# First layer of a four-layer program: reloads of the weights issued two units ahead, and each half's moves put on one queue

## The chip, the cores and the metric

The kernel runs on one core of one Trainium2 chip. The time is the device time of one execution in microseconds (us). For the kernel before it is 3445.14 us, the median of three runs (3443.86 to 3448.17).

## What is computed

The program chains four layers. The change touches the first alone, an attention over projected columns:

```python
def _L0_xattn_ref(z1ss, u1ss, Wqkv0, Wqkv1, Winj0, Winj1, Wo, bo, r_w_bias):
    for i in range(2):                       # columns 0:256 and 256:512
        h = jnp.einsum('od,bdl->bol', Wq_list[i], z1ss[:, :, s:e])
        h = h + jnp.einsum('od,bdl->bol', Wi_list[i], u1ss[:, :, s:e])
    q, k, v = jnp.split(w_heads, 3, axis=1)  # 16 heads of 64
    rq = q + r_w_bias[None, :, :, None]
    score = jnp.einsum('bndi,bndj->bnij', rq, k) * SCALE
    prob = jax.nn.softmax(score, axis=-1)
    attn_vec = jnp.einsum('bnij,bndj->bndi', prob, v)
    attn_out = jnp.einsum('od,bdl->bol', Wo, attn_vec) + bo[None, :, None]
    x = attn_out + z1ss
    return (x - m) * jax.lax.rsqrt(var + LN_EPS)
```

Here x is 8 x 256 x 512 in float32. The other three layers (a recurrent mixing layer, two attentions with a perceptron, a non-local block) run after it and are the same in both kernels.

## The kernel before

The function `l0_attention` works through 64 units. A unit n is one pair of heads (8 pairs) of one batch (8 batches). Batches go in four turns of two lanes, and the order of the units is turn, pair, lane: `where(n)` gives (turn bp, pair, lane l). All products are split into a high and a low part of float32r, so the weights of one pair are two tiles of 1 MB, `w_hi` and `w_lo` (two buffers each, by the pair's parity), and the weights for the values of two pairs are `wv_hi` and `wv_lo` (1 MB each, one buffer).

**Weights.** In turn 0 SyncE loads the raw weights, ScalarE and VectorE split them, and SyncE stores both parts to HBM (`split_weights`, L318 to L331). For turns 1 to 3 ScalarE reloads the parts (`load_w`, L685). A pair is counted over all turns as t = 8 bp + pair; its projection of q and k (L419) runs one unit ahead, inside unit 2t - 1. Before, the high parts (of `w`, and for even t of `wv`) are issued in unit 2t - 3 and the low parts in unit 2t - 2, both behind the second pair of exponentials.

**Turning the probabilities.** A unit's probabilities are made in two halves f = 0, 1 (two blocks of 128 rows each). VectorE transposes 32 x 32 blocks inside a half (L778), and 16 DMAs, called pieces here, move blocks between partitions from `prob` to `probT` (`move`, L270). A piece is 64 KB. Halves are numbered i = 2n + f and three buffers go round (`RING`). A piece may be issued when the half is transposed (`turned`) and the product that read the same `probT` buffer three halves ago is complete. Before, nine of a half's 16 pieces are issued by SyncE and seven by GpSimd. `half_moved` waits for both, on TensorE ahead of the product with the values (`weigh_values`, L478) and on ScalarE ahead of writing a `prob` buffer again (`exponentials`, L576).

**Order on each engine.** Each engine has one program in a fixed order. In unit n:

- TensorE: scores of blocks 0 and 1 (L453), projections of q and k for unit n + 1 (L419), scores of blocks 2 and 3, the turned row sums of unit n - 1 (L462), the output projection of n - 2 (L492), the product with the values of n - 1 (L478; first half, then second half, into one bank), and where pair is even the values of unit n + 1 (L437).
- ScalarE: exponentials of blocks 0 and 1, `q_hi` of n + 1 (L599), other copies, exponentials of blocks 2 and 3, the reload issues, the copy `oT` of the product of n - 1 (L612).
- GpSimd: scaling of the product of n - 2 (L380, waits for ScalarE's `oT`), the row sums of n - 1 (L375), the pieces of half 1 of unit n - 1, the pieces of half 0 of unit n.
- SyncE: its pieces of half 0 and of half 1 of unit n; then in turn 0, lane 0, `split_weights` of the next pair; loads of x and loads and stores of `acc` where a turn begins or ends.

GpSimd's pieces of half 1 of unit n thus stand behind the scaling of the product of unit n - 1. DMAs that ScalarE issues appear on queue q10 of the profile, SyncE's on q1, GpSimd's on q0.

Of the kernel before, what the change touches and what calls it, by code (L numbers as in the profile page):

```python
# [6 lines left out]
F32 = mybir.dt.float32  # L7
# [11 lines left out]
LANES = 2  # L19
TURNS = B // LANES  # L20
# [134 lines left out]
def l0_attention(nc, kept, first, d, x, u, att, x1):  # L155

    D, HP = 64, 8
# [3 lines left out]
    RING = 3  # L161
# [3 lines left out]
    QUADS = HP // 2  # L165
    MOVES = [(g, r) for g in range(Q) for r in range(Q)]
    BY_SP = 9
    H2 = range(2)
# [30 lines left out]
    w_scratch = [scratch(f"kept_w_{part}", (HP, P, KT, 2, 2, P)) for part in ("hi", "lo")]  # L199
    wv_scratch = [scratch(f"kept_wv_{part}", (QUADS, P, KT, 2, 2, P)) for part in ("hi", "lo")]  # L200

    with Phase(nc, "l0") as ph:
# [4 lines left out]
        w_hi, w_lo = [[ph.sb(f"w_{part}{i}", [P, KT, 2, 2, P], F32R) for i in range(2)] for part in ("hi", "lo")]  # L207
# [57 lines left out]
        def half_moved(eng, i):  # L265

            eng.wait_ge(moved_sp[i % RING], 16 * BY_SP * (i // RING + 1))
            eng.wait_ge(moved_pool[i % RING], 16 * (len(MOVES) - BY_SP) * (i // RING + 1))

        def move(eng, n, f, pieces, moved):  # L270

            i = 2 * n + f
            eng.wait_ge(turned, IT * n + 2 * f + 2)
            if i >= RING:
                full(eng, S[f"o{(i - RING) // 2}"])
            elif i == 1:
                eng.wait_ge(wv_lo_ready, 1)
            elif i == 2:
                eng.wait_ge(wo_lo_ready, 1)
            for g, r in pieces:  # L280
                eng.dma_start(probT[i % RING][r * SQ:(r + 1) * SQ, g, :, :, :, :],  # L281
                              prob[i % RING][g * SQ:(g + 1) * SQ, r * IT:(r + 1) * IT, :, :, :]).then_inc(moved[i % RING], 16)

        def projected(eng, n):

            full(eng, S[f"v{n}_1"] if where(n)[1] % 2 == 0 else S[f"k{n}"])

        with ph.block() as block:
            @block.sync
            def _(sp):  # L290
# [43 lines left out]
                for n in range(HALF):  # L334
                    bp, pair, l = where(n)
                    move(sp, n, 0, MOVES[:BY_SP], moved_sp)
                    move(sp, n, 1, MOVES[:BY_SP], moved_sp)
                    if bp == 0 and l == 0 and pair + 1 < HP:
# [23 lines left out]
            def _(pool):  # L362
# [19 lines left out]
                for n in range(HALF + 2):  # L382
# [4 lines left out]
                    if 0 < n <= HALF:  # L387
                        move(pool, n - 1, 1, MOVES[BY_SP:], moved_pool)
                    if n >= HALF:
                        continue  # L390
                    move(pool, n, 0, MOVES[BY_SP:], moved_pool)
                    if n == VAR + 1:
# [174 lines left out]
            def _(act):  # L567
# [116 lines left out]

                def load_w(t, part):  # L685
                    p, i = t % HP, t % 2
                    projected(act, LANES * (t - 2) + 1)
                    if i == 0:
                        act.wait_ge(wv_stored, 32 * QUADS)
                        act.dma_start((wv_hi, wv_lo)[part][:, :, :, :, :].bitcast(F32), wv_scratch[part][p // 2]).then_inc(wv_in, 16)  # L690
                    act.wait_ge(w_stored[i], 32 * QUADS)
                    act.dma_start((w_hi, w_lo)[part][i][:, :, :, :, :].bitcast(F32), w_scratch[part][p]).then_inc(w_in[i], 16)

# [14 lines left out]
                for n in range(HALF):  # L708
                    bp, pair, l = where(n)
                    exponentials(n, (0, 1))  # L710
                    if n + 1 < HALF:
                        queries(n + 1)
# [6 lines left out]
                    exponentials(n, (2, 3))  # L719
                    t = (n - 1) // LANES + 2  # L720
                    if HP <= t < TURNS * HP:
                        load_w(t, 1 - l)
                    if n == 0:
# [2507 lines left out]
```

## Time and profile before

| what | value |
|---|---|
| median of three runs | 3445.14 us (3443.86 to 3448.17) |
| the profiled execution | 3442.56 us |
| its span, first to last instruction | 3440.5 us |
| mean granted clock of TensorE | 0.949 |
| TensorE matmul busy | 3115.6 us, 91% |
| VectorE busy | 2362.2 us, 69% |
| ScalarE busy | 1742.2 us, 51% |
| GpSimd busy | 701.2 us, 20% |
| the first layer's 64 units | from the start to about 1302 us |

The page gives busy time by engine over the whole span; the first layer is a third of it. Rows of the trace name the line and the tile that an instruction writes and reads, what the engine waited for ahead of it, and for DMAs the time from issue to landing. "PE" is TensorE, "DVE" VectorE, "ACT" ScalarE, "POOL" GpSimd, "SP" SyncE; a "q" behind the name is the engine's sequencer, which issues DMAs.

### The profile page before, as it was taken

The numbers are of one execution on the slowest core, as the hardware profiler recorded it, in microseconds if no ns is written. First come the engines' busy times: TensorE is split into PE (matmuls) and PEld (weight loads), VectorE is DVE, ScalarE is ACT, GpSimd is POOL, SyncE is SP. The second block draws the span as 40 slices with busy tenths as digits, with TensorE's granted clock in tenths as the row PEclk, the third lists the DMA queues.
The fourth block names the chain that finished last, engine by engine and source line by source line (L and its number), as shares of the span: only waits on it lengthen the run. The fifth ranks groups of instructions, "written<-read, shape, count | busy, mean of one in ns | idle before, by whom it ended". The sixth has DMA issues, their size and how long they took to land. (4 is left out here: it accounts for less than half of the span.)

```text
span 3440.5 us, 55581 instructions
## 1 busy us (share of the span) xinstructions
PE 3115.6 (91%) x20384; PEld 2400.2 (70%) x20384; DVE 2362.2 (69%) x3589; ACT 1742.2 (51%) x4185; POOL 701.2 (20%) x1207
## 2 busy tenths in 40 slices
PE   7998999999998996799999997589999999699998
PEld 6777777777777774566666664378887787488885
DVE  6776666666675662999999999257777888543212
ACT  4454444544454543355566553247777777432222
POOL 2444444544444441000000000011101111000000
PEclk9999999999999998899999998789999999899999
DMA  7668766666675655445555444210011110310004
GB/s 245 209 218 268 225 184 183 207 212 197 197 234 162 207 143 187 121 96 123 116 117 120 104 109 104 59 64 14 26 56 56 44 44 29 108 50 12 25 13 167
DMA packets 179676, 434.78 MB, mean 126 GB/s; under 512 B 52912, under 2 KB 61104, under 8 KB 154960
## 3 DMA queue, kind: packets, MB, share of 16 engines
q1 hardware_dynamic: 120256, 262.17, 26.9%
q10 hardware_dynamic: 28304, 106.09, 8.6%
q0 software_dynamic: 30848, 62.97, 7.3%
q8 instruction: 164, 2.69, 0.3%
q14 instruction: 104, 0.85, 0.1%
HBM read 233.95 MB, written 62.91 MB: 86 GB/s over the span
## 5 line engine op out<-in xcount | busy, mean ns | idle before, releaser
L281 POOL DMA_DIRECT2D l_probT<-l_prob x896 | 441.2, 500 | 258.6 <-DVE l_prob L778 238.8
L756 DVE TENSOR_REDUCE l_nmax<-l_bank 128x1 f32<-128x512 f32 x512 | 317.0, 681 | 198.2 <-PE l_bank L453 198.2
L576 ACT ACTIVATE l_prob<-l_bank,l_nmax 128x512 f32<-128x512 f32 x512 | 344.5, 688 | 135.1 <-DVE l_nmax L756 120.5
L419 PE MATMUL l_bank<-l_x_hi,l_w_hi 128*128 128x256 f32 x1024 | 307.6, 300 | 75.4 <-DMA l_w_lo<-kept_w_lo 54.5
L778 DVE STREAM_TRANSPOSE l_prob<-l_prob 128x1024 f32<-128x1024 f32 x256 | 314.4, 1228 | 16.3 <-DVE l_acc L799 9.7
L419 PE MATMUL l_bank<-l_x_hi,l_w_lo 128*128 128x256 f32 x1024 | 299.8, 293 | 0.0
L419 PE MATMUL l_bank<-l_x_lo,l_w_hi 128*128 128x256 f32 x1024 | 299.0, 292 | 0.0
L1817 DVE TENSOR_TENSOR_SCAN l_kv<-l_wx,l_kv 128x2056 f32<-128x2056 f32 x64 | 283.8, 4435 | 3.1 <-DVE l_sxc L1938 1.5
L419 PEld LDWEIGHTS l_bank<-l_x_hi,l_w_hi 128*128 128x128 f32 x1024 | 207.0, 202 | 99.5 <-DMA l_w_lo<-kept_w_lo 59.2
L2391 ACT ACTIVATE l2a_sc<-l2a_sc,l2a_nmax 128x256 f32<-128x256 f32 x512 | 254.7, 508 | 41.1 <-DVE l2a_nmax L2507 41.1
L478 PE MATMUL l_bank<-l_probT,l_v 128*64 128x256 f32 x2048 | 248.6, 397 | 25.9 <-issue 12.5
L478 PEld LDWEIGHTS l_bank<-l_probT,l_v 128*64 128x64 f32 x2048 | 147.9, 142 | 121.6 <-issue 44.0
L2507 DVE CUSTOM_DVE_ANT_0 l2a_sc<-l2a_sc,l2a_mb 128x256 f32<-128x256 f32 x512 | 217.1, 484 | 0.0
L419 PEld LDWEIGHTS l_bank<-l_x_hi,l_w_lo 128*128 128x128 f32 x1024 | 207.1, 202 | 0.0
L419 PEld LDWEIGHTS l_bank<-l_x_lo,l_w_hi 128*128 128x128 f32 x1024 | 206.7, 202 | 0.0
L2500 DVE SCALAR_TENSOR_TENSOR l2a_sc<-l2a_bank,l2a_m 128x512 f32<-128x512 f32 x256 | 158.7, 681 | 54.1 <-PE l2a_bank L2263 54.1
L380 POOL TENSOR_TENSOR l_oT<-l_oT,l_rT 128x512 f32<-128x512 f32 x64 | 99.8, 1559 | 455.5 <-ACT l_oT L612 455.5
L2871 DVE TENSOR_TENSOR l2b_h_lo<-l2b_hf,l2b_h_hi 128x512 fp32r<-128x512 f32 x64 | 44.0, 691 | 199.3 <-ACT l2b_h_hi L2814 199.3
L2807 ACT ACTIVATE l2b_hf<-l2b_bank,l2b_b 128x512 f32<-128x512 f32 x64 | 44.0, 688 | 255.4 <-PE l2b_bank L2749 255.4
L1809 DVE TENSOR_TENSOR l_kv<-l_vb,l_ik 128x2048 f32<-128x2048 f32 x64 | 145.9, 2279 | 6.4 <-DMA l_vb<-vd 5.9
L437 PE MATMUL l_bank<-l_wv_hi,l_x_hi 128*128 128x256 f32 x512 | 148.1, 289 | 1.9 <-DVE l_wv_lo L815 1.9
L2274 PE MATMUL l2a_bank<-l2a_ident,l2a_sc 128*128 128x128 f32 x1024 | 133.2, 277 | 16.6 <-DVE l2a_oT L2520 8.7
(348 smaller groups left out, 7989.3 us busy)
## 6 DMA issues: line engine op xcount, KB each, us to landing
l_probT<-l_prob SPq DMA_DIRECT2D x1152, 64.0 KB, 2.7
l_vb<-vd SPq DMA_DIRECT2D x64, 1024.0 KB
l_probT<-l_prob POOLq DMA_DIRECT2D x896, 64.0 KB, 2.4
l_w_hi<-kept_w_hi ACTq DMA_DIRECT2D x24, 1024.0 KB, 7.2
l_w_lo<-kept_w_lo ACTq DMA_DIRECT2D x24, 1024.0 KB, 7.7
l_wv_hi<-kept_wv_hi ACTq DMA_DIRECT2D x12, 1024.0 KB, 5.4
l_wv_lo<-kept_wv_lo ACTq DMA_DIRECT2D x12, 1024.0 KB, 5.6
kept_w_hi<-l_w_hi SPq DMA_DIRECT2D x8, 1024.0 KB, 9.8
```

Of the source, the lines that this page charges most:

```text
L281: eng.dma_start(probT[i % RING][r * SQ:(r + 1) * SQ, g, :, :, :, :], prob[i % RING][g * SQ:(g + 1) * SQ, r * IT:(r + 1) * IT, :, :, :]).th ...
L419: mm = pe.matmul(s.ap[:, c * ROWS:(c + 1) * ROWS], a[:, kt, c, g, :], b[:, kt, c * ROWS:(c + 1) * ROWS], start=m == 0, stop=m == 3 * KT - 1)
L437: mm = pe.matmul(s.ap[:, at], a[:, kt, jt * P:(jt + 1) * P], b[:, kt, c, :, :], start=m == 0, stop=m == 3 * KT - 1)
L478: mm = pe.matmul(s.ap[own, f * ROWS:(f + 1) * ROWS], v[l][:, pair % 2, j, own], half[:, :, :, j, h, :], start=j == 0, stop=j == IT - 1)
L576: act.activation(prob[i % RING][:, :, it % 2, h, :].rearrange("p (q t) s -> p t q s", q=Q), s.ap[:, :].rearrange("p (t q s) -> p t q s", t ...
L756: dve.tensor_reduce(nmax[:, n % 2, it, h:h + 1], s.ap[:, :], AX.X, ALU.max, negate=True).then_inc(max_ready, 1)
L778: dve.transpose(own, own).then_inc(turned, 1)
L1809: dve.tensor_tensor(kv[n % NK][:, :, 1:ROWS + 1], vb[n % NV][:, :, :], ik[:, ct, :].unsqueeze(1).to_broadcast([P, NJ, ROWS]), ALU.mult).th ...
L1817: dve.tensor_tensor_scan(own, wx[:, :, :].rearrange("p j t -> p (j t)"), own, 0.0, ALU.mult, ALU.add)\
L2391: ins = act.activation(to[:, r, :], to[:, r, :], ACT.Exp, scale=-1.0, bias=nmax[:, k % SC_RING, i, r:r + 1], accum_out=rsum[:, k % SC_RING ...
L2500: dve.scalar_tensor_tensor(out=sc[k % SC_RING][i][:, :, :], in0=s.ap[:, :].rearrange("p (r j) -> p r j", r=RT), scalar=HD ** -0.5, in1=own ...
L2507: dve.tensor_tensor_reduce(out=to[:, r, :], in0=to[:, r, :], in1=own[:, r, :], scale=-1.0, scalar=3.0e38, op0=ALU.add, op1=ALU.min, accum_ ...
```

## The change

Two things. First, `half_moved`, `move` and their calls: the 16 pieces of every half 0 are issued by SyncE and the 16 pieces of every half 1 by GpSimd. Second, the reloads: `w_hi` and `w_lo` of pair t are issued together in unit 2t - 3, and `wv_hi` and `wv_lo`, for even t, together in unit 2t - 2, both behind the first pair of exponentials instead of the second. What a half waits for, the bytes moved and all other instructions stay.

```diff
-            eng.wait_ge(moved_sp[i % RING], 16 * BY_SP * (i // RING + 1))
-            eng.wait_ge(moved_pool[i % RING], 16 * (len(MOVES) - BY_SP) * (i // RING + 1))
-
-        def move(eng, n, f, pieces, moved):
+            eng.wait_ge((moved_sp, moved_pool)[i % 2][i % RING], 16 * len(MOVES) * (i // (2 * RING) + 1))
+
+        def move(eng, n, f, moved):
...
-            for g, r in pieces:
+            for g, r in MOVES:
...
-                    move(sp, n, 0, MOVES[:BY_SP], moved_sp)
-                    move(sp, n, 1, MOVES[:BY_SP], moved_sp)
+                    move(sp, n, 0, moved_sp)
...
-                        move(pool, n - 1, 1, MOVES[BY_SP:], moved_pool)
+                        move(pool, n - 1, 1, moved_pool)
                     if n >= HALF:
                         continue
-                    move(pool, n, 0, MOVES[BY_SP:], moved_pool)
...
-                def load_w(t, part):
+                def load_w(t):
                     p, i = t % HP, t % 2
                     projected(act, LANES * (t - 2) + 1)
-                    if i == 0:
-                        act.wait_ge(wv_stored, 32 * QUADS)
-                        act.dma_start((wv_hi, wv_lo)[part][:, :, :, :, :].bitcast(F32), wv_scratch[part][p // 2]).then_inc(wv_in, 16)
                     act.wait_ge(w_stored[i], 32 * QUADS)
-                    act.dma_start((w_hi, w_lo)[part][i][:, :, :, :, :].bitcast(F32), w_scratch[part][p]).then_inc(w_in[i], 16)
+                    for part, to in enumerate((w_hi, w_lo)):
+                        act.dma_start(to[i][:, :, :, :, :].bitcast(F32), w_scratch[part][p]).then_inc(w_in[i], 16)
+
+                def load_wv(g):
+                    projected(act, LANES * 2 * (g - 1) + 1)
+                    act.wait_ge(wv_stored, 32 * QUADS)
+                    for part, to in enumerate((wv_hi, wv_lo)):
+                        act.dma_start(to[:, :, :, :, :].bitcast(F32), wv_scratch[part][g % QUADS]).then_inc(wv_in, 16)
...
                     exponentials(n, (0, 1))
+                    t = (n - 1) // LANES + 2
+                    if HP <= t < TURNS * HP:
+                        if l == 1:
+                            load_w(t)
+                        elif t % 2 == 0:
+                            load_wv(t // 2)
...
                     exponentials(n, (2, 3))
-                    t = (n - 1) // LANES + 2
-                    if HP <= t < TURNS * HP:
-                        load_w(t, 1 - l)
```

The order of ScalarE's instructions in a unit with an even t and in the one behind it, before (`l_prob` rows are exponentials, `l_q_hi` the query of the next unit):

```order
L576 ACTIVATE l_prob,l_rsum<-l_bank,l_nmax 128x4x4x32 x4
L690 DMA l_wv_hi<-kept_wv_hi 128x2048
L692 DMA l_w_hi<-kept_w_hi 128x2048
L612 ACTIVATE l_oT<-l_bank 128x512
L576 ACTIVATE l_prob,l_rsum<-l_bank,l_nmax 128x4x4x32 x4
L599 ACTIVATE l_q_hi<-l_bank,l_rb 128x512
L618 ACTIVATE l_oT_hi<-l_oT 128x512
L583 ACTIVATE l_k_hi<-l_bank 128x512
L605 ACTIVATE l_rT<-l_bank 128x512
L576 ACTIVATE l_prob,l_rsum<-l_bank,l_nmax 128x4x4x32 x4
L690 DMA l_wv_lo<-kept_wv_lo 128x2048
L692 DMA l_w_lo<-kept_w_lo 128x2048
```

And with the change, from the first exponentials of the same unit on:

```order
L572 ACTIVATE l_prob,l_rsum<-l_bank,l_nmax 128x4x4x32 x4
L686 DMA l_w_hi<-kept_w_hi 128x2048
L686 DMA l_w_lo<-kept_w_lo 128x2048
L595 ACTIVATE l_q_hi<-l_bank,l_rb 128x512
L614 ACTIVATE l_oT_hi<-l_oT 128x512
L579 ACTIVATE l_k_hi<-l_bank 128x512
L601 ACTIVATE l_rT<-l_bank 128x512
L572 ACTIVATE l_prob,l_rsum<-l_bank,l_nmax 128x4x4x32 x4
L608 ACTIVATE l_oT<-l_bank 128x512
L572 ACTIVATE l_prob,l_rsum<-l_bank,l_nmax 128x4x4x32 x4
L692 DMA l_wv_hi<-kept_wv_hi 128x2048
L692 DMA l_wv_lo<-kept_wv_lo 128x2048
```

Both parts of `w` now stand a half unit earlier than the high part did, and `wv` stands alone behind the first exponentials of the next unit.

SyncE's order in turn 0, from the pieces of units 1 and 2 to the pieces behind the stores and loads of pair 2, before:

```order
L281 DMA l_probT<-l_prob 32x512 x36
L322 DMA kept_wv_hi<-l_wv_hi 128x2048
L323 DMA kept_wv_lo<-l_wv_lo 128x2048
L326 DMA l_xraw<-in_l_wv 128x2048
L329 DMA first_anx<-in_l_wqk 128x2048
L330 DMA kept_w_hi<-l_w_hi 128x2048
L331 DMA kept_w_lo<-l_w_lo 128x2048
```

With the change:

```order
L279 DMA l_probT<-l_prob 32x512 x32
L320 DMA kept_wv_hi<-l_wv_hi 128x2048
L321 DMA kept_wv_lo<-l_wv_lo 128x2048
L324 DMA l_xraw<-in_l_wv 128x2048
L327 DMA first_anx<-in_l_wqk 128x2048
L328 DMA kept_w_hi<-l_w_hi 128x2048
L329 DMA kept_w_lo<-l_w_lo 128x2048
```

The 36 pieces were nine of each half of units 1 and 2; the 32 are all of half 0 of the same units, so the six transfers of 1 MB no longer stand behind a piece of unit 2's half 1.

GpSimd's order in one unit, before:

```order
L380 TENSOR_TENSOR l_oT<-l_oT,l_rT 128x512
L375 COPY l_rows<-l_rinv 128x512
L281 DMA l_probT<-l_prob 32x512 x14
```

With the change:

```order
L377 TENSOR_TENSOR l_oT<-l_oT,l_rT 128x512
L372 COPY l_rows<-l_rinv 128x512
L279 DMA l_probT<-l_prob 32x512 x16
```

The 14 pieces were seven of half 1 of the unit before and seven of half 0 of this one; the 16 are all of half 1 of the unit before.

## Rows read from the trace of the kernel before

**Rows 1.** Stretches: busy time by engine, granted clock, DMA share, GB/s, of turns 2 to 4

```profile
338.00:1220.00 882.00, 818.41 (x6173) 670.13 (x6173) 587.66 (x809) 418.18 (x1001) 392.89 (x709) 0.96 0.67 200
```

**Rows 2.** TensorE's waits in the first layer: us in total, times, longest

```profile
PE l_bank L419 <- DMA l_w_lo<-kept_w_lo: 54.5, 11, 6.8
PE l_bank L478 <- issue: 12.5, 3, 5.1
```

**Rows 3.** Timeline, TensorE: start, us, line, operation, wait before it

```profile
725.37 0.58 PE L419 MATMUL l_bank<-l_x_hi,l_w_hi 128*128 128x256 f32 x1 [6.83 <-DMA l_w_lo<-kept_w_lo]
```

**Rows 4.** Timeline, ScalarE, starts of `l_q_hi` around that wait

```profile
692.20 0.69 ACT L599 ACTIVATE l_q_hi<-l_bank,l_rb 128x512 fp32r<-128x512 f32 x1 [0.18 <-PE l_bank L419]
706.92 0.69 ACT L599 ACTIVATE l_q_hi<-l_bank,l_rb 128x512 fp32r<-128x512 f32 x1 [0.20 <-PE l_bank L419]
730.90 0.69 ACT L599 ACTIVATE l_q_hi<-l_bank,l_rb 128x512 fp32r<-128x512 f32 x1 [9.46 <-PE l_bank L419]
```

**Rows 5.** Stretches, behind a reload wait

```profile
803.00:806.40 3.40, 3.25 (x15) 3.25 (x16) 0.09 (x1) 0.00 (x0) 3.23 (x8) 0.52 1.06 263
```

**Rows 6.** Timeline, GpSimd, second half of unit 37

```profile
785.03 3.47 POOL L281 DMA_DIRECT2D l_probT<-l_prob  x7
```

**Rows 7.** Timeline, TensorE, product of unit 37

```profile
793.57 3.67 PE L478 MATMUL l_bank<-l_probT,l_v 128*64 128x256 f32 x32
```

**Rows 8.** Timeline, ScalarE, unit 38

```profile
784.24 0.69 ACT L576 ACTIVATE l_prob<-l_bank,l_nmax 128x512 f32<-128x512 f32 x1 [1.08 <-DVE l_nmax L756]
...
792.77 0.68 ACT L576 ACTIVATE l_prob<-l_bank,l_nmax 128x512 f32<-128x512 f32 x1
...
793.91 0.33 ACTq L690 DMA_DIRECT2D l_wv_lo<-kept_wv_lo  x1
```

**Rows 9.** GpSimd's pieces of 743 to 747.5 us, no reload in flight

```profile
DMA to landing us min/median/max: 2.1/2.2/2.3
```

**Rows 10.** GpSimd's pieces of 876 to 880 us and of 1239.5 to 1241.6 us

```profile
DMA to landing us min/median/max: 4.2/4.4/7.0
...
DMA to landing us min/median/max: 2.2/3.3/6.6
```

**Rows 11.** DMA queues, 871.5 to 878.5 us: packets, MB, share of 16 engines

```profile
q10 hardware_dynamic: 276, 2.05, 84.1%
```

**Rows 12.** DMA queues, 1242.2 to 1244.2 us

```profile
q10 hardware_dynamic: 80, 0.66, 85.2%
...
q0 software_dynamic: 9, 0.00, 0.8%
```

**Rows 13.** DMA queues, 413 to 417 us

```profile
q0 software_dynamic: 280, 0.58, 57.0%
```

**Rows 14.** SyncE's pieces of 740 to 747 us: ns min/median/max, starts

```profile
L281 SPq DMA_DIRECT2D l_probT<-l_prob x9: 507/591/596, 741.6 to 746.6; - x9
```

**Rows 15.** Timeline, GpSimd, behind the 119th piece after the last pause

```profile
722.31 0.98 POOL L281 DMA_DIRECT2D l_probT<-l_prob  x2 [1.84 <-issue]
```

**Rows 16.** Timelines of SyncE, VectorE, GpSimd and TensorE, unit 2

```profile
94.07 0.58 SPq L322 DMA_DIRECT2D kept_wv_hi<-l_wv_hi  x1
...
83.44 2.29 DVE L810 TENSOR_TENSOR l_w_lo<-first_anx,l_w_hi 128x2048 fp32r<-128x2048 f32 x1 [1.75 <-ACT l_w_hi L631]
...
88.38 3.46 POOL L281 DMA_DIRECT2D l_probT<-l_prob  x7 [0.73 <-DVE l_prob L778]
...
96.03 3.67 PE L478 MATMUL l_bank<-l_probT,l_v 128*64 128x256 f32 x32
```

**Rows 17.** DMA queue q0, 96 to 114 us; landing of GpSimd's pieces, 93 to 107 us

```profile
q0 software_dynamic: 382, 0.78, 14.5%
...
DMA to landing us min/median/max: 1.9/7.5/10.4
```

**Rows 18.** Timelines of GpSimd and TensorE, last unit

```profile
1293.18 3.47 POOL L281 DMA_DIRECT2D l_probT<-l_prob  x7
...
1299.78 1.95 PE L478 MATMUL l_bank<-l_probT,l_v 128*64 128x256 f32 x16 [0.56 <-DMA l_probT<-l_prob]
```

More of the change, by code:

```diff
@@ L166, in l0_attention @@
     MOVES = [(g, r) for g in range(Q) for r in range(Q)]
-    BY_SP = 9
     H2 = range(2)
```

## The prediction

> **What bounds the kernel now.** I first read the table of busy time by stretches. In the turns that reload their weights TensorE is busy 818 of 882 us and its granted clock is 0.96 of 2.4 GHz, while the DMA engines are busy two thirds of the time [rows 1]. So the change can give back TensorE's idle time and the lost clock, and it can take more of both. Next, TensorE's waits: 54.5 us, in 11 waits, are for the reload `l_w_lo<-kept_w_lo`, and 12.5 us, in 3, are at the product of the moved probabilities (L478, "issue") [rows 2]. The longest reload wait is 6.83 us [rows 3]. What one wait costs is seen in the starts of `l_q_hi`, one per unit: 14.7 us between two of them where TensorE never waits, 24.0 us over the longest wait [rows 4]. That is 9.3 us for 6.8 us of wait. The rest is the clock: after the wait of 799 to 803 us the next 3.4 us are granted 0.52, nearly all at 1.2 GHz [rows 5].
>
> **Part 1, reloads earlier.** The order shows it: `w_hi` and `w_lo` are issued together, two units before their first use, and the two `wv` pieces a unit later. They were landing within some 12 us and now have two units, 29 us, from issue to use, so the ten large waits go. Gain: 54.5 us, plus the clock, 2.5 us (9.3 - 6.8) on the longest wait and 1.6 us on the window shown (half of 3.4), say 2.1 us ten times: **-76 us**. The added issues on ScalarE cost nothing: one takes 0.33 us while exponentials are still queued [rows 8], and ScalarE waits for TensorE afterwards.
>
> **Part 2, second halves on GpSimd alone.** GpSimd issues 7 pieces in 3.47 us, 0.496 us each [rows 6]; 16 pieces end their issue 7.44 us after the first one. Take unit 37. GpSimd may start only at 785.03, since scaling and row sums stand ahead of it (SyncE, which had nine of the pieces, has no such step ahead). TensorE's product starts at 793.57 and needs the second half in its middle, at 795.4 [rows 7]. The last piece is issued at 792.5, so it must land within 2.9 us. Pieces that meet no other traffic land in 2.1 to 2.3 us [rows 9]: 0.6 us to spare. Pieces that meet a reload and its backlog took up to 7.0 us, and up to 6.6 us in another place [rows 10].
>
> Which of the two applies? In the changed order a reload of 2 MB is issued after the first exponentials of the next unit, which start at 784.24 [rows 8]; in the old place the issue came 1.1 us after the start, so now at 785.4, with GpSimd's first piece. A reload fills the DMA engines: 84% for 7 us [rows 11]. While it does, GpSimd's queue q0 gets almost nothing: 0.8% of the time against 85% for q10, with three GpSimd pieces waiting [rows 12]. So about 13 of the 16 pieces wait until the reload is over, at 785.4 + 1.6 + 5.9 (2.05 MB at that share) = 793. Beside SyncE's queue q0 then moves 0.58 MB in 4 us, 0.45 us a piece [rows 13]: 13 pieces need 5.9 us, the end is about 799, a landing of 6.5 to 7. The bounds are 2.3 us (no lateness) and 10.4 us, the longest landing under a burst [rows 17]; I take 7.0, measured behind a reload, the nearest row: 4.1 us late.
>
> The Trainium skill ("DMA: Bandwidth & Descriptors", Queues, rings and completion order) says that a DMA engine goes round the queue rows that have work, packet by packet. By that rule q0 would get a turn in every round, and its pieces would be one to two us late instead of four; the stretch just named speaks against it. The same page (Rules for kernel authors) says that spreading DMAs over engines gains no bandwidth and saves issue time only; the 7.44 us above are that issue time, which this change stops spreading.
>
> How often: TensorE projects values for units 0 and 1 of every four, which gives those second halves slack. Units 1 and 2 of four have none between, and in both the new order has a reload in flight (`wv` in one, the odd `w` in the other). The chain product, ScalarE copy, GpSimd scaling, 16 pieces, product then closes on itself: it takes 14.1 us plus what the landing exceeds 2.3 us, against 14.7. So both units pay 4.1 us, and the clock once (2.1, the other one hides in the chain): 10.3 us for four units, in 12 groups: **+124 us**.
>
> First halves, all on SyncE, cost nothing: 16 pieces of 0.59 us [rows 14] and a landing of 7 take 16 us, and ScalarE and TensorE want them about one unit and the exponentials, 19 us, after they are turned. The cover is gone if a landing reaches 10 us.
>
> **Smaller terms.** (a) GpSimd's issue pauses after every 119 pieces or so, 1.5 to 3 us, one shown [rows 15]: eight pauses, now all in second halves, half of them in tight units: +8. (b) First turn: in SyncE's order the store-and-load burst of 5 to 6 MB now stands ahead of the second half. It was issued at 94.07 and is now free when `w_lo` is made, at 85.7; GpSimd's pieces start at 88.38 and are wanted at 97.9 [rows 16]. Under the burst q0 moves 0.78 MB in 18 us, 0.66 pieces per us [rows 17], the burst lasts some 21 us, so 11 pieces are through at 107 and the rest at 109.4: 11.5 us late, twice, and 8 for the smaller third burst, plus clock 6: 37. It removes the three waits of 12.5 us and their clock of 6. Net +18, and +4 for unit 0: +22. If q0 got its turn the net would be about -5. (c) The last two units have no projection ahead: for the last, 1293.18 + 9.7 against 1299.78, 3 us [rows 18], the one before some 2: +5. (d) In units 49 to 53 the normalisation of a first tile makes TensorE wait anyway; that can hide the lateness of two units: -8.
>
> **Sum.** -76 + 124 + 8 + 22 + 5 - 8 = +75 us, on the profiled execution's 3442.6 us: 3518. The median of the runs shown is 2.6 us above that execution, so I forecast **3520 us**.
>
> **The rivals.**
> *Fair turns* (the other side). GpSimd's pieces get a turn between the reload's packets. The reload's 276 packets are 17 for each of 16 engines, 5.9 / 17 = 0.35 us; a piece of q0 takes 57% of 0.45, 0.26 us [rows 11, 13]. At 0.61 us a piece instead of 0.496, 13 pieces fall back by 1.5 us, with SyncE's some 2: they land in 4 to 4.6 us and are 1.7 us late at most, taken as too short to drop the clock. 24 x 1.7 = 41, pauses 4, first turn -5, tail 5, (d) -4: -76 + 41 = -35, 3410 us. It decides from a landing of about 4.5 us downwards. For it: many pieces land in 2.1 to 2.3 us [rows 9]. Against it: those met no reload, and q0 had 0.8% where one ran [rows 12]. The skill's rule above is this rival.
> *No contention.* The reload's packets miss the pieces, nothing is late: -76 + 5 + 3 - 10 = -78, 3367 us. Against it: the issues coincide within 0.5 us.
> *Longer backlog.* Reload, first half and second half pile up, landing 10 us (10.4 under the burst [rows 17]): 12 x (2 x 7.1 + 2.1) = 196, total +147, 3592 us.
> *The reload is not moved.* The order excludes it; a reload could still land late under its own backlog, but it has 25 us.
>
> **How the numbers follow.** Main case (landing 6 to 8 us, 3490 to 3550) 0.53, longer backlog 0.11, fair turns 0.22, no contention 0.07, and 0.07 between fair turns and the main case, which is near no change. A measurement of this kernel can tell 0.2%, 7 us. Faster 0.29, same 0.05, slower 0.66. The range leaves out the case without contention, the lowest of fair turns and the worst of the backlog: 3400 to 3590.
>
> **What would show it.** In the changed profile the wait for `l_w_lo<-kept_w_lo` is gone; in its place TensorE waits at the product of `l_probT` for `DMA l_probT<-l_prob` or "issue", about 24 times, 4 us each, two in every four units, and two or three waits over 8 us before 300 us. GpSimd's last pieces in those units land after 6 us or more. The mean granted clock is not above 0.949. I am wrong if those waits are under 2 us, or if GpSimd's queue holds a third of the DMA time while a reload runs.

## The result, and the profile after

The changed kernel takes 3598.4 us, median of four runs (3595.9 to 3604.1), where the kernel before takes 3444.5 (3443.2 to 3448.2): a ratio of 1.0447 (95% interval 1.0429 to 1.0465), 154 us slower. Forecast were 75 us slower, 3520, with a range up to 3590. The sign and the places are as predicted, the size is twice as large, and 3598 is 8 us above the range.

Two lines of the page after: busy time by engine, and the product's group (busy us, mean ns of one, idle before it).

```profile
PE 3157.4 (88%) x20384; PEld 2404.1 (67%) x20384; DVE 2362.0 (66%) x3589; ACT 1743.4 (48%) x4185; POOL 754.9 (21%) x1335
...
L474 PE MATMUL l_bank<-l_probT,l_v 128*64 128x256 f32 x2048 | 298.3, 448 | 200.7 <-DMA l_probT<-l_prob 190.2
```

L474 is L478 of before. TensorE's busy time was 3115.6 us and is now 3157.4 for the same matmuls: it ran slower for part of them. The same stretch of units as [rows 1], in the table of busy time by stretches (columns as there):

```profile
364.00:1352.00 988.00, 845.83 (x6169) 668.68 (x6170) 588.62 (x810) 419.26 (x1003) 433.29 (x809) 0.93 0.66 179
```

It takes 988 us where it took 882, TensorE is idle for 142 us of it instead of 64, and the granted clock is 0.93 instead of 0.96. TensorE's waits over the span (us, times, longest):

```profile
PE l_bank L474 <- DMA l_probT<-l_prob: 190.2, 34, 11.1
```

The wait for `l_w_lo<-kept_w_lo` of [rows 2] is gone, and this one stands in its place. One of the waits, unit 37, on three timelines of the kernel after. TensorE:

```profile
879.81 1.95 PE L474 MATMUL l_bank<-l_probT,l_v 128*64 128x256 f32 x16
888.85 3.68 PE L474 MATMUL l_bank<-l_probT,l_v 128*64 128x256 f32 x16 [7.09 <-DMA l_probT<-l_prob]
```

GpSimd, and the time from issue to landing of its pieces of 871 to 879.2 us:

```profile
871.27 7.86 POOL L279 DMA_DIRECT2D l_probT<-l_prob  x16
...
DMA to landing us min/median/max: 1.9/8.9/10.2
```

ScalarE:

```profile
872.26 0.33 ACTq L692 DMA_DIRECT2D l_wv_hi<-kept_wv_hi  x1
872.62 0.46 ACTq L692 DMA_DIRECT2D l_wv_lo<-kept_wv_lo  x1
873.47 0.69 ACT L595 ACTIVATE l_q_hi<-l_bank,l_rb 128x512 fp32r<-128x512 f32 x1 [0.21 <-PE l_bank L415]
...
892.58 0.60 ACT L608 ACTIVATE l_oT<-l_bank 128x512 f32<-128x512 f32 x1 [10.78 <-PE l_bank L474]
...
897.45 0.69 ACT L595 ACTIVATE l_q_hi<-l_bank,l_rb 128x512 fp32r<-128x512 f32 x1 [0.19 <-PE l_bank L415]
```

The reload is issued 1 us after GpSimd's first piece, as forecast. The last of the 16 pieces, issued at 878.6, lands at 888.8. The product's second half then takes 3.68 us where its first half took 1.95. ScalarE's `oT`, which GpSimd scales before it may issue again, follows at 892.6, and the next `l_q_hi` comes 24.0 us after the last. The same interval took 20.6 us in the kernel before, with its reload wait, and takes 14.7 where nothing waits. Stretches of the end of that wait and of the product behind it:

```profile
886.00:889.00 3.00, 0.15 (x2) 0.15 (x4) 0.00 (x0) 0.00 (x0) 0.00 (x0) 0.53 0.76 182
889.00:892.00 3.00, 3.00 (x16) 1.56 (x16) 0.00 (x0) 0.00 (x0) 0.00 (x0) 0.50 0.01 3
```

After 7 us of idling the granted clock is 0.50, the 1.2 GHz level, and it holds through this product. What the queues did meanwhile (packets, MB, share of 16 engines), 873 to 882, 882 to 886 and 886 to 888.8 us:

```profile
q10 hardware_dynamic: 278, 2.08, 77.3%
q0 software_dynamic: 191, 0.39, 15.2%
q1 hardware_dynamic: 80, 0.12, 5.2%
```

```profile
q0 software_dynamic: 261, 0.52, 56.1%
q1 hardware_dynamic: 288, 0.40, 46.3%
```

```profile
q1 hardware_dynamic: 390, 0.52, 77.2%
q0 software_dynamic: 17, 0.02, 3.7%
```

While the reload (q10) runs, GpSimd's q0 gets 15%, not the 0.8% of [rows 12]; then it shares with SyncE's q1; and its last 17 packets come through only among 390 of q1, which are the first half of the next unit (SyncE issues it from 874.6 to 886.0).

The first turn. SyncE, GpSimd and TensorE at unit 2, and TensorE at unit 6:

```profile
87.39 0.58 SPq L320 DMA_DIRECT2D kept_wv_hi<-l_wv_hi  x1
```

```profile
90.51 7.90 POOL L279 DMA_DIRECT2D l_probT<-l_prob  x16 [0.73 <-DVE l_prob L781]
```

```profile
111.09 1.54 PE L474 MATMUL l_bank<-l_probT,l_v 128*64 128x256 f32 x5 [11.01 <-DMA l_probT<-l_prob]
...
198.97 1.12 PE L474 MATMUL l_bank<-l_probT,l_v 128*64 128x256 f32 x4 [11.12 <-DMA l_probT<-l_prob]
```

The burst that stood at 94.07 [rows 16] is issued at 87.4, ahead of GpSimd's pieces.

For every kernel of this study the first layer can be cut at the starts of `l_q_hi` (one per unit, as in [rows 4]). "End" is the end of the layer's last product. "Product waits" is TensorE's idle time ahead of the product with the values in the middle stretch. Each row is one profiled execution; those of e2, e4 and e12 were the slowest of their four, 8, 13 and 7 us above the median.

| kernel | units 0-15 | units 16-47 | 48 to end | end | product waits |
|---|---|---|---|---|---|
| before | 321.7 | 623.8 | 338.7 | 1301.7 | 0 |
| after | 347.1 | 707.3 | 381.2 | 1453.1 | 103.3 |
| e7, no reloads | 335.9 | 582.0 | 337.1 | 1272.3 | 9.9 |
| e9, late slot, 9/7 | 317.8 | 582.3 | 327.9 | 1245.6 | 8.4 |
| e3, late slot, 16/16 | 338.6 | 602.5 | 341.8 | 1300.1 | 25.1 |
| e2, early slot, 9/7 | 324.9 | 654.3 | 350.3 | 1347.0 | 61.6 |
| e1, old slot, 16/16 | 340.1 | 620.3 | 352.1 | 1329.9 | 17.1 |
| e4, queues swapped | 343.4 | 705.5 | 383.3 | 1449.2 | 100.6 |
| e10, half the reload | 343.2 | 644.0 | 353.5 | 1357.5 | 60.5 |
| e11, `wv` later | 343.5 | 664.3 | 372.1 | 1397.0 | 76.9 |
| e8, wait filled | 346.2 | 695.7 | 386.6 | 1445.7 | 38.7 |
| e5, spread, 16/16 | 344.5 | 611.1 | 348.4 | 1321.4 | 35.2 |
| e6, spread, 9/7 | 326.2 | 598.4 | 344.7 | 1285.9 | 21.9 |
| e12, spread, 9/7, `wv` later | 318.6 | 595.1 | 335.9 | 1266.8 | 16.6 |

Nearly all of the loss is in the first layer: its end moved by 151.4 us, the total by 154.

### The profile page after: what moved, and what is told of

The parts are those of the page before. It is cut to its first block and busy times, and to the rows that moved or that the text cites. A ratio compares the mean times of both kernels' runs of the same rounds, so it can differ in the third digit from the quotient of the medians.

```text
span 3595.6 us, 55378 instructions
## 1 busy us (share of the span) xinstructions
PE 3157.4 (88%) x20384; PEld 2404.1 (67%) x20384; DVE 2362.0 (66%) x3589; ACT 1743.4 (48%) x4185; POOL 754.9 (21%) x1335
## 5 line engine op out<-in xcount | busy, mean ns | idle before, releaser
L279 POOL DMA_DIRECT2D l_probT<-l_prob x1024 | 503.2, 500 | 19.2 <-issue 13.4
L474 PE MATMUL l_bank<-l_probT,l_v 128*64 128x256 f32 x2048 | 298.3, 448 | 200.7 <-DMA l_probT<-l_prob 190.2
L474 PEld LDWEIGHTS l_bank<-l_probT,l_v 128*64 128x64 f32 x2048 | 160.0, 159 | 324.8 <-DMA l_probT<-l_prob 203.2
L415 PE MATMUL l_bank<-l_x_hi,l_w_hi 128*128 128x256 f32 x1024 | 298.6, 292 | 18.5 <-DVE l_x_lo L850 11.6
L415 PE MATMUL l_bank<-l_x_hi,l_w_lo 128*128 128x256 f32 x1024 | 291.6, 285 | 0.0
L415 PE MATMUL l_bank<-l_x_lo,l_w_hi 128*128 128x256 f32 x1024 | 291.3, 284 | 0.0
L415 PEld LDWEIGHTS l_bank<-l_x_hi,l_w_hi 128*128 128x128 f32 x1024 | 198.0, 193 | 41.8 <-issue 34.8
L608 ACT ACTIVATE l_oT<-l_bank 128x512 f32<-128x512 f32 x64 | 38.3, 599 | 344.4 <-PE l_bank L474 344.4
L415 PEld LDWEIGHTS l_bank<-l_x_hi,l_w_lo 128*128 128x128 f32 x1024 | 198.3, 194 | 0.0
L415 PEld LDWEIGHTS l_bank<-l_x_lo,l_w_hi 128*128 128x128 f32 x1024 | 198.2, 194 | 0.0
L2810 ACT ACTIVATE l2b_hf<-l2b_bank,l2b_b 128x512 f32<-128x512 f32 x64 | 44.1, 689 | 255.0 <-PE l2b_bank L2752 255.0
## 6 DMA issues: line engine op xcount, KB each, us to landing
l_wv_lo<-kept_wv_lo ACTq DMA_DIRECT2D x12, 1024.0 KB, 11.5
```

The costliest lines, as they stand in the source:

```text
L415: mm = pe.matmul(s.ap[:, c * ROWS:(c + 1) * ROWS], a[:, kt, c, g, :], b[:, kt, c * ROWS:(c + 1) * ROWS], start=m == 0, stop=m == 3 * KT - 1)
L474: mm = pe.matmul(s.ap[own, f * ROWS:(f + 1) * ROWS], v[l][:, pair % 2, j, own], half[:, :, :, j, h, :], start=j == 0, stop=j == IT - 1)
```

## The experiments

The theory (A) is that of the prediction: in two of every four units a 2 MB reload stands beside the second half's pieces, and TensorE waits for them. Each run's ratio is against the kernel before on the same chip, where that took 3443.7 to 3446.0 us; A, B, C and D in the expectations are the theories that each of them names. "Old slot" is where the reloads were, "early slot" where the change puts them (behind the first exponentials), "late slot" the same pairs behind the second exponentials of the same unit.

### One part of the change at a time: e1 and e2

e1 takes the change of queues alone:

```diff
-                    move(sp, n, 0, MOVES[:BY_SP], moved_sp)
-                    move(sp, n, 1, MOVES[:BY_SP], moved_sp)
+                    move(sp, n, 0, moved_sp)
...
-                    move(pool, n, 0, MOVES[BY_SP:], moved_pool)
```

> Each half on one queue, reloads as before (high part two units ahead, low part one unit ahead, both behind the second exponentials). Theory A, coincidence: the change is slow because GpSimd's 16 second-half pieces have 0.6 us to spare and the reload is issued with their first piece. Here the reload is issued 6 us ahead of that piece, so the halves are late by 0 to 1.6 us; the reload waits stay, the first turn costs 25 us and the last units 10: 3480 to 3510 us. Rival B, one queue alone: 16 pieces on GpSimd cost 8.7 us in each tight unit whatever the reload does, and the reload waits stay beside it: 3600 us or more. Rival C, reload alone: the queues do nothing, 3445.

Measured: 3475.0 us, ratio 1.0087 (1.0068 to 1.0107). TensorE's waits:

```profile
PE l_bank L474 <- DMA l_probT<-l_prob: 67.6, 21, 12.2
PE l_bank L415 <- DMA l_w_lo<-kept_w_lo: 29.2, 10, 4.6
```

The loss is that of the first turn (+18 us) and of the end; units 16 to 47 are no slower than before (620.3 and 623.8): 17.1 us of product waits came, and the reload waits fell from 54.5 to 29.2. The median is 5 us below A's interval.

e2 takes the change of reloads alone, with nine and seven pieces as before:

```diff
                     exponentials(n, (0, 1))
+                    t = (n - 1) // LANES + 2
+                    if HP <= t < TURNS * HP:
+                        if l == 1:
+                            load_w(t)
+                        elif t % 2 == 0:
+                            load_wv(t // 2)
```

> Reloads two units ahead, the pieces of each half 9 to SyncE and 7 to GpSimd as before. Theory A: the second half is issued by 788.5 in unit 37's times, before the reload fills the engines, so it is late by 0 to 1 us, and the reload waits (54.5 us and 21 us of clock) go: 3365 to 3395 us. Rival B says the same. Rival C, the new place of the reload alone makes the halves late: 3445 us or more, with product waits of several us in two of four units.

Measured: 3485.6 us, ratio 1.0108 (1.0080 to 1.0136). Its waits:

```profile
PE l_bank L478 <- DMA l_probT<-l_prob: 62.8, 20, 9.0
PE l_bank L478 <- issue: 30.3, 5, 10.0
```

A was wrong here. The reload waits are gone, and yet the kernel is 42 us slower: the early slot costs in itself, whichever queues carry the pieces. Part 1 was costed at -76 with nothing on the other side; the collision was charged to Part 2 alone. The two parts together cost more (154) than the sum of each alone (31 + 42): the 16 pieces of one queue and the reload in the early slot make each other worse.

### The slot: e3, e9

e3 is the changed kernel with the same reloads in the late slot (its edit is shown); e9 is that slot with nine and seven pieces:

```diff
                     exponentials(n, (0, 1))
-                    t = (n - 1) // LANES + 2
-                    if HP <= t < TURNS * HP:
-                        if l == 1:
-                            load_w(t)
-                        elif t % 2 == 0:
-                            load_wv(t // 2)
...
                     exponentials(n, (2, 3))
+                    t = (n - 1) // LANES + 2
+                    if HP <= t < TURNS * HP:
+                        if l == 1:
+                            load_w(t)
+                        elif t % 2 == 0:
+                            load_wv(t // 2)
```

> The changed kernel with both reload pairs issued behind the second exponentials of the same units instead of the first, some 9 us later and 6 us ahead of the second half of that unit. Nothing else differs. Theory A: the product waits fall from 7 us to 0 to 2 us: 3410 to 3460 us. Rival B: no difference from the changed kernel, 3590 to 3600 us.

Measured: 3448.2 us, ratio 1.0012 (1.0002 to 1.0023). Half a unit later, with the same bytes, queues and number of DMAs, 150 of the 154 us are gone. Its product waits of 400 to 1220 us:

```profile
PE l_bank L474 <- DMA l_probT<-l_prob: 27.7, 15, 4.5
```

They are 1.8 us in the mean, as A expects, but the longest is above its 2 us.

> The kernel before with the reloads two units ahead in whole pairs, but behind the second exponentials. Theory A (the reload's place beside tight second-half pieces made the earlier reload slow; nine and seven pieces keep the first turn fast): no reload wait, first turn 322 to 327 us, units 16 to 47 in 590 to 605 us; 3400 to 3435 us, faster than both kernels. Rival C (any early reload costs the split pieces as much as it gains): 3445 or more.

Measured: 3389.7 us, ratio 0.9855 (0.9830 to 0.9880). That goes the way that A expects, and further: 10 us below its interval, with 317.8 us for the first turn and 582.3 for units 16 to 47, both below what A gave them. This version beats both kernels, by 55 us and 209 us. Its stretch answering to [rows 1], and its product waits:

```profile
335.00:1164.00 829.00, 802.20 (x6151) 651.10 (x6151) 587.76 (x811) 418.05 (x1003) 396.32 (x715) 0.99 0.72 213
```

```profile
PE l_bank L478 <- issue: 18.3, 5, 5.3
...
PE l_bank L478 <- DMA l_probT<-l_prob: 5.2, 3, 2.6
```

TensorE is idle for 27 us of 829 and the clock is at 0.99. Against e2, the same kernel with the early slot, units 16 to 47 are 72 us shorter; against e3, which has the other division of queues, 20.

### Is it the reload, and how much of it: e7, e10, e11

e7 is the changed kernel without the reloads. It leaves out the transfers and TensorE's waits for them, so turns 1 to 3 use the weights that turn 0 left.

```diff
-                    t = (n - 1) // LANES + 2
-                    if HP <= t < TURNS * HP:
-                        if l == 1:
-                            load_w(t)
-                        elif t % 2 == 0:
-                            load_wv(t // 2)
```

> The changed kernel without the weight reloads of turns 1 to 3 (it leaves out those transfers and the waits for them, so later turns multiply by the first turn's last weights). Theory A (the reload beside the second half makes nearly all the loss; the second halves in one queue cost little by themselves): the product waits of units 16 to 47 shrink under 1 us each, the quads of units 16 on come down from 81.7 to about 73 us; the first turn keeps its loss of 18 to 25 us. About 3400 us (3375 to 3430). Rival C (sixteen pieces in one queue are late by issue alone, reload or not): over 3480 us, with waits of 2 us or more in units n%4 of 1 and 2.

Measured: 3415.1 us, ratio 0.9915 (0.9896 to 0.9934). Units 16 to 47 fall from 707.3 to 582.0. In these units GpSimd's longer issue costs nothing without a reload: e9, with nine and seven pieces, takes 582.3. Waits of 400 to 1220 us:

```profile
PE l_bank L470 <- DMA l_probT<-l_prob: 7.8, 8, 2.4
```

e10 leaves the high parts (1 MB) in the early slot and puts the low parts (1 MB) in the late one:

```diff
                     exponentials(n, (0, 1))
...
-                            load_w(t)
+                            load_w(t, 0)
...
                     exponentials(n, (2, 3))
...
+                            load_w(t, 1)
```

> The changed kernel with the hi parts of each reload (1 MB) left behind the first exponentials and the lo parts (1 MB) behind the second ones. Theory A (what counts is how many bytes stand in the DMA engines ahead of the second half's pieces): 1 MB less is about 4.5 us less, the landings in the tight units fall from about 10 to 5 or 6 us and the waits from 6.5 to 2 or 3 us: units 16 to 47 in 640 to 665 us, 3490 to 3540 us. Rival C (once a reload is there at all, the second half is stopped for as long as any backlog lasts, and it closes on itself): landings 8 us or more, 3570 to 3600. Rival D (the second MB, now under the next unit's pieces, only moves the wait): landings short, but waits at the first half's product, over 3550.

Measured: 3498.4 us, ratio 1.0172 (1.0138 to 1.0206); units 16 to 47 in 644.0. GpSimd's pieces of unit 37 (landing), and the queues around them (831 to 838 us):

```profile
DMA to landing us min/median/max: 2.1/5.3/6.0
```

```profile
q10 hardware_dynamic: 144, 1.05, 46.6%
q0 software_dynamic: 287, 0.59, 35.7%
```

A's landing and time hold; TensorE's waits in the tight units are 3.8 us (60.5 / 16, one of them 11.6), more than its 2 or 3. The second MB costs 63.3 us over 16 tight units (707.3 less 644.0), 4.0 us each. For the first MB the price depends on what stands for none: 62.0 us, 3.9 each, against no reload at all (e7, 582.0), but 41.5 us, 2.6 each, against both MB in the late slot (e3, 602.5). The second comparison keeps the bytes the same, as e10 too has 1 MB in the late slot. So more bytes ahead of the half cost more time, but that each MB costs the same is not shown.

e11 moves the `wv` pair alone, to the late slot of the same unit; the `w` pairs stay:

```diff
                     exponentials(n, (0, 1))
-                        elif t % 2 == 0:
-                            load_wv(t // 2)
...
                     exponentials(n, (2, 3))
+                    if HP <= t < TURNS * HP and t % 2 == 0 and l == 0:
+                        load_wv(t // 2)
```

> The changed kernel with the wv pair alone moved, to behind the second exponentials of the unit that follows; the w pairs stay behind the first exponentials. Theory A (two coincidences in four units, each with its own price of about 8.7 us): the wait in units 1 of four goes (intervals 29 to 21 us), that in units 2 of four stays (23.5 us and 6 us of wait): 12 times 8.7 is 104 us, so 3480 to 3520 us. Rival C (one coincidence left is enough to slow the whole closed chain): 3560 or more. Rival D (the wait in the second unit was a consequence of the first): under 3460.

Measured: 3538.7 us, ratio 1.0291 (1.0265 to 1.0316), 19 us above A's interval and 21 below rival C's. Landings of unit 37 (which meets no reload now) and of unit 38 (which still does):

```profile
DMA to landing us min/median/max: 1.9/2.3/2.9
```

```profile
DMA to landing us min/median/max: 6.3/9.4/9.8
```

The wait of unit 37 is gone, that of unit 38 has grown from 7.0 to 7.9 us. Over the eight units of its kind in 16 to 47 the mean grew from 5.9 to 9.0 us, 25 us in all, so these units got 43 us back, not the 70 that A gives to that place (8 times 8.7). The cause of the growth was not separated: `wv_lo` of the late slot lands at 860.3, after `w` is issued at 857.6, and at unit 38 GpSimd starts its pieces 1.1 us late after a pause of its own.

### Is it GpSimd's queue: e4

```diff
-            eng.wait_ge((moved_sp, moved_pool)[i % 2][i % RING], 16 * len(MOVES) * (i // (2 * RING) + 1))
+            eng.wait_ge((moved_pool, moved_sp)[i % 2][i % RING], 16 * len(MOVES) * (i // (2 * RING) + 1))
...
-                    move(sp, n, 0, moved_sp)
+                    move(sp, n, 1, moved_sp)
...
+                    move(pool, n, 0, moved_pool)
```

> The changed kernel with the queues swapped: all pieces of first halves on GpSimd, of second halves on SyncE. SyncE starts 2 us sooner and issues at 0.59 us a piece, so its last piece is issued 0.6 us sooner. Theory A (any queue is starved while a reload runs): second halves late by 4 to 6 us, first turn as before the change: 3500 to 3560 us. Rival D (only GpSimd's queue is starved by the reload): late by 0 to 1 us, 3380 to 3410 us.

Measured: 3586.3 us, ratio 1.0419 (1.0390 to 1.0448). With the second halves on SyncE and the first ones on GpSimd TensorE's waits are 180.6 us, against 190.2:

```profile
PE l_bank L473 <- DMA l_probT<-l_prob: 180.6, 37, 11.1
```

So the prediction's picture of a queue q0 that is starved as against the others does not hold: TensorE waits as long whichever of the two queues carries the second half.

### What the clock costs: e8

e8 puts work into the wait, three more products of the first half:

```diff
                     for f in range(2):
+                        if f and n >= 12 and n % 4 in (1, 2):
+                            for again in range(3):
+                                for j in range(IT):
+                                    for h in H2:
+                                        own = slice(D * h, D * h + D)
+                                        pe.matmul(s.ap[own, ROWS:2 * ROWS], v[l][:, pair % 2, j, own], half[:, :, :, j, h, :],
+                                                  start=j == 0, stop=j == IT - 1)
                         half_moved(pe, 2 * n + f)
```

> The changed kernel with the product of the first half made three times more in the tight units from 12 on (48 matmuls, some 5.4 us, whose result is written again with the same values), ahead of the wait for the second half. It takes no transfer away. Theory A (the second half is late by its transfers alone and TensorE's idle time also costs half the clock afterwards, within the closed chain): the product of the second half takes 1.8 us again instead of 3.7, the intervals fall by about 2 to 3 us each in some 24 units: 3530 to 3560 us, 40 to 70 below the changed kernel, though TensorE does more work. Rival C (the clock loss is beside the chain, only the late transfer counts): 3590 to 3605 us, as before. Rival D (the extra product itself delays the chain, as TensorE was not truly free): over 3610.

Measured: 3596.3 us, ratio 1.0434 (1.0404 to 1.0464), the time of the changed kernel. Unit 37 on TensorE:

```profile
877.12 5.35 PE L474 MATMUL l_bank<-l_probT,l_v 128*64 128x256 f32 x48
882.90 1.95 PE L481 MATMUL l_bank<-l_probT,l_v 128*64 128x256 f32 x16 [0.43 <-DMA l_probT<-l_prob]
```

The clock is back (0.98 in the stretch of 364 to 1345 us instead of 0.93) and the product takes 1.95 us again, but units 16 to 47 are only 11.6 us shorter, and the units behind them 5.4 longer. Units 16 to 47 in the table of stretches, the changed kernel, e7 and e8:

```profile
364.62:1071.90 707.28, 603.71 (x4418) 477.71 (x4417) 422.83 (x581) 297.39 (x708) 309.28 (x578) 0.92 0.66 179
353.20:935.20 582.00, 570.25 (x4418) 463.01 (x4417) 422.00 (x581) 296.57 (x710) 315.47 (x582) 1.00 0.52 132
363.40:1059.10 695.70, 656.96 (x5187) 520.26 (x5186) 422.98 (x581) 297.15 (x709) 309.98 (x579) 0.99 0.67 182
```

The low clock costs 33.5 us of TensorE's busy time in the changed kernel (603.7 against 570.2 for the same matmuls). Less its 16 fillers of 5.35 us, e8 is busy for 571.4, so it has all of that back, 32.3 us. But fillers and waits together are 124.3 us in which the product's second half was not there, against 103.3 in the changed kernel: 21 of the 32 us went into waiting for it. My expectation of 40 to 70 us was wrong, and the time is that of rival C. I read it so that the transfers set the pace in these units and a faster TensorE meets them earlier.

### Other places for the reloads: e5, e6, e12

e5 (16 and 16 pieces) and e6 (nine and seven) put each reload where a chain of four units has slack; the lines that both add are shown. e12 is e6 with `wv` one unit later (`l == 0` in place of `l == 1` in its condition):

```diff
                     exponentials(n, (0, 1))
+                    if HP <= t < TURNS * HP and (t % 2 == 0) == (l == 1):
+                        load_w(t)
...
                     exponentials(n, (2, 3))
+                    if HP <= t < TURNS * HP and t % 2 == 0 and l == 1:
+                        load_wv(t // 2)
```

> The changed kernel with the three reload pairs put where the chain has slack: w of odd units behind the first exponentials of n%4==0, w of even ones behind the first exponentials of n%4==1, wv behind the second exponentials of n%4==1. Theory A (only a reload that runs beside the second-half pieces of n%4 1 and 2 costs): no reload wait, quads from unit 16 on of 73 to 77 us, 3400 to 3460. Rival C (any reload beside any half's pieces costs; the place matters little): 3500 us or more.

> The kernel before (nine pieces on SyncE, seven on GpSimd, every half) with the reloads at the same three slack places as in the run with one queue for each half. Theory A (split pieces are done issuing 3 us sooner and the first turn keeps its speed, reload waits gone): 3380 to 3430, faster than both kernels. Rival C (the earlier reloads delay the pieces by as much as they gain, as the run with the reloads alone did): 3445 to 3490.

> The kernel of the spread reloads with nine and seven pieces, with the wv pair moved from behind the second exponentials of units 1 of four to those of units 2 of four, so that in units 17, 33 and 49 it doesn't meet the even w pair and the accumulators' store and load. Theory A (the three stretched units of 26.5 us were that meeting): those intervals return to 20.7 us, 12 to 18 us gained: 3405 to 3425. Rival C (it meets the pieces of units 2 of four there and costs elsewhere what it gains): 3425 to 3450.

Measured: e5 3469.6 (1.0071, 1.0051 to 1.0092), 10 us above A's interval; e6 3428.0 (0.9952, 0.9933 to 0.9971) and e12 3406.9 (0.9903, 0.9880 to 0.9926), both within it. All avoid the collision and are 129 to 192 us faster than the changed kernel, and all are slower than e9, whose placement is plainer. For e12 A had the time right and the reason wrong: the three units near the start of a turn that took 26.5 to 27.0 us in e6 (17, 33, 49) still take 27.5 to 29.4. What e12 gained lies elsewhere and was not followed further.

## Why the prediction was right, and where it was wrong

**Right: what goes and what comes.** The direction and the mechanism hold. The wait for `l_w_lo` is gone. Product waits came in two of every four units and in the first turn, 34 in all; landings are above 6 us; the clock fell (0.934 over the span, 0.949 before). e7, e3 and e9 show that the coincidence of reload and second half is the cause: each takes it away, and units 16 to 47 come down from 707.3 to 582.0, 602.5 and 582.3 us.

**Wrong, the main step: "I take 7.0, measured behind a reload, the nearest row: 4.1 us late".** The last piece took 10.2 us to land in unit 37, where TensorE waited 7.1 us, and over units 16 to 47 it waited 103.3 us at the product, 6.5 us in each of 16 tight units. In the prediction's terms the half is complete 14 us after GpSimd's first piece (799 - 785), and it was 17.5 (888.8 - 871.3). The reload was to be over after 8 us; it held 77% of the engines until 882, 10.7 us after the first piece, while q0 and q1 took another 20% beside it. Behind it 5.9 us were reckoned, and it took 6.8, the last 2.8 of them for 17 packets among 390 of SyncE's next first half. What that first half adds by itself was not tested. The total to be moved, 2 MB of reload, 1 MB of this half and 1 MB of the next, was there in the rows; the step let the reload run as if alone. Its 5.9 us "at that share" are 84% of the 7 us of [rows 11], which is the reload with the engines to itself; at that share the row gives 7 us, and the same sum ends 1.1 us later. The 7.0 of [rows 10] came from a reload that met seven or eight pieces of GpSimd, not sixteen.

That is the rival of the longer backlog (landing 10 us, 3592 us), to which I had given 0.11, with a row that bore it out [rows 17] quoted in the text. Its landing is right; that its time comes within 7 us of the measured one is in part luck, as it has 76 us for Part 1 where 56 came, and 196 for the lateness where the reloads in the early slot cost 181.

**Wrong, the same step's other side: Part 1 had nothing against its gain, and the collision stood in Part 2 alone.** e2 has no Part 2, and the early slot still costs it 72 us in units 16 to 47 (654.3 against e9's 582.3), with 61.6 us of product waits. The prediction has no term for nine and seven pieces that meet the moved reload.

**Wrong, a smaller step: "the clock once (2.1, the other one hides in the chain)".** Against e7, units 16 to 47 lost 125.3 us, of which 93.4 are more product waits (103.3 less 9.9). The 31.9 that are left are 2.0 us for each tight unit, and TensorE's busy time is 33.5 us longer for the same matmuls, so the clock (3.68 us for 1.95 in the row) is paid in both. A group of four lost 15.7 us (125.3 / 8) where 10.3 stood: 11.7 for lateness and 4.0 for the rest, instead of 8.2 and 2.1. e8 shows, though, that only 11.6 of these 32 us can be had back by themselves.

**Part 1, -76.** e9 gives what the early reload is worth without a collision: 55 us by the medians, 56 in the first layer. Of it 41.5 are in units 16 to 47. In two of those intervals, a few units into a turn, e9 takes 26.2 and 27.9 us for the 20.7 and 20.9 of before, which is 12.5 us given back; there `wv` comes in beside SyncE's loads and stores of x and the accumulators, and its pieces stand behind them in the queue. That this is the cause was not tested. With them it would be 6.8 us a group, against 6.3 (76 / 12) forecast. So the price of a wait was right.

**Nearly right: the first turn, +22.** The waits of 11.0, 11.1 and 9.75 us at units 2, 6 and 10 are near those forecast ("11.5 us late, twice, and 8 for the smaller third burst"). Units 0 to 15 took 25.4 us more, but 11.2 of them are gone without the reloads (e7), in units 12 to 15 where the first ones run; they belong to Part 2. The burst itself cost 14 to 18 us (e7 +14.2, e3 +16.9, e1 +18.4). All kernels with a half on one queue need 336 to 347 us for these units, all with nine and seven 318 to 326.

**Smaller terms.** (a) Pauses of GpSimd: 13.4 us in 10 for the whole changed run, most of them 1.1 us, where the kernel before had 19.6 us in 26; how much of it lay on the path was not tested. (c) From the last `l_q_hi` to the end of the last product it takes 43.7 us (1453.1 - 1409.4) for 32.8: +10.9 for a term of 5. (d) Units 52 to 55 take 95.1 us for 95.3: the normalisation hides the lateness of both tight units, 15.7 us where 8 was taken.

**Rivals.** "Fair turns" said that q0's pieces would move between the reload's packets at 0.61 us each. q0 got 15% during the reload, more than the 0.8% of [rows 12] and far less than a third, and the landing was 10 us: it fell.

The Trainium skill ("DMA: Bandwidth & Descriptors", Queues, rings and completion order) has each DMA engine go round the queue rows that have work, packet by packet. The trace agrees with it only in part: from 873 to 882 us q0 had 191 packets and q10 278, not as many. At one packet each, q0's 2.0 KB (0.39 MB / 191) beside q10's 7.5 KB would be 21% of their bytes, an estimate; it had 16% (0.39 of 2.47 MB). Whether the profile's packets are those of the page no run here shows. What I made of the rule, 0.61 us a piece, was further off. The Trainium skill (same page, Rules for kernel authors) also says that issuing from several engines brings no bandwidth. e4, which only swaps the two issuing engines, fits it, with 3586 us against 3598.

The first layer's sum, in the terms of the prediction: Part 1 -56 (e9 less before), the reloads beside the second halves +181 (11.2 + 125.3 + 44.1, the changed kernel less e7 in the three stretches) and one queue for each half +27 (e7 less e9, of it 18 in the first turn and 9 after unit 47). These are the steps from the kernel before over e9 and e7 to the changed kernel, so they must add up to the 151 by which the layer's end moved. They stood at -76, +124 and (with all smaller terms) +27. Other steps would divide it otherwise, for the parts act on each other: one queue for each half costs 27 us without reloads, 54.5 with them in the late slot (e3 less e9) and 106 with them in the early one (after less e2).

## What to carry to other kernels

- Before a large transfer is put earlier, list what small transfers are due in its new place, and for each chain that closes on a DMA add up the bytes of all queues that are in flight there. Here the second MB cost 4.0 us in each tight unit and the first 2.6 to 3.9, and half a unit of shift was worth 150 us.
- Test each half of a double change alone: both cost 31 and 42 us, together 154, and the good half was one shift away from a gain of 55.
- When a quoted row gives a worse value for a landing, ask whether the change makes its conditions the common case, before a milder row is taken.

## What was not expected of the hardware

- The landing of a half is set by its last packets. In unit 37 q0 moved 0.91 MB of the half from 873 to 886 us (0.39 + 0.52), and the last 17 packets needed 2.8 us more among 390 of another queue.
- A busier TensorE did not make the kernel faster while a transfer was late: with 0.98 of the clock instead of 0.93 (e8) the medians are 2 us apart.
- The queue made little difference: with the second halves on SyncE's queue TensorE waited 180.6 us for them, with them on GpSimd's 190.2.
